# Second attention of a fused block: next queries scaled before the last two tiles' sums, row roots merged with query roots, shared tiles joined in pairs

## What is computed

```
x = x + tanh(g_xattn[0]) * attention0(layernorm(x), ctx)
x = x + tanh(g_ffn[0])   * (routed64(layernorm(x)) + shared(layernorm(x)))
x = x + tanh(g_xattn[1]) * attention1(layernorm(x), ctx)      # the stage changed
x = x + tanh(g_ffn[1])   * mixture8(layernorm(x))

# attention1, 16 heads of 16, keys of 48 + 16 positions, softmax over each part apart
q = ln(x @ Wq + bq);  k = ln(y @ Wk + bk);  v = y @ Wv + bv
ctx = softmax(q k^T / 4) v  +  softmax(q k_dca^T / 4) v_dca
out = ctx @ Wo + bo
```

## Time and profile before

| | us |
|---|---|
| median of 3 runs | 1215.48 (1213.35 to 1218.72) |
| the profiled execution | 1215.52 |
| its span in the trace | 1213.8 |
| busy in it: PE, DVE, ACT, POOL | 953.3, 721.6, 430.7, 279.5 |

### The profile page before, as it was taken

The page is one execution under the profiler, slowest core; times in us unless marked ns, Lnnn a source line. Parts: engine busy times, 40 slices in busy tenths (PEclk is TensorE's granted clock), DMA queues, the critical chain, the costliest instruction groups (busy, mean ns, idle before and its releaser), DMA issues.

```text
span 1213.8 us, 16300 instructions
## 1 busy us (share of the span) xinstructions
PE 953.3 (79%) x5499; PEld 794.4 (65%) x5499; DVE 721.6 (59%) x1685; ACT 430.7 (35%) x809; POOL 279.5 (23%) x225
## 2 busy tenths in 40 slices
PE   5998998989986630576767755777868999999998
PEld 3876867867865520465656632544547989999898
DVE  7267667577478989222222468988986445444343
ACT  4546455454563410111111104355354232332322
POOL 0323303304300000588888720101100000000000
PEclk9999998999989765777787857887869999999899
DMA  8004000000000141578887655000000000000000
GB/s 293 4 1 150 2 1 1 1 1 1 1 1 1 44 123 41 121 167 181 177 184 165 115 132 204 1 3 1 1 1 1 1 18 2 1 17 0 18 1 18
DMA packets 58945, 66.48 MB, mean 55 GB/s; under 512 B 5069, under 2 KB 55687, under 8 KB 58119
## 3 DMA queue, kind: packets, MB, share of 16 engines
q1 hardware_dynamic: 45236, 46.45, 12.4%
q0 software_dynamic: 12288, 18.88, 8.8%
q10 hardware_dynamic: 1363, 0.37, 0.1%
HBM read 48.13 MB, written 17.56 MB: 54 GB/s over the span
## 4 chain that ended last, share of the span: by engine, by line
PE 49%; DVE 19%; issue 13%; DMA 6%; ACT 6%; POOL 6%; ACTq 0%; DVEq 0%; POOLq 0%
PE bank L2039 12%; PE bank L2065 7%; PE bank L1737 4%; DMA acc<-y,dst_now 4%; PE bank L1692 4%; PE bank L1722 3%; PE bank L1926 3%; POOL acc L507 2%; PE bank L2050 2%; DMA xg<-table,src_now 2%; POOL q_lo L486 2%; POOL xg L497 2%; DVE cand L919 2%; PE bank L1713 2%; DVE keyT L922 2%
## 5 line engine op out<-in xcount | busy, mean ns | idle before, releaser
L2039 PE MATMUL bank<-gu_hi,xnT_split 128*128 128x352 f32 x640 | 164.0, 330 | 4.9 <-DVE soft L1235 3.7
L486 POOL TENSOR_TENSOR q_lo<-soft,q_hi 128x512 fp32r<-128x512 f32 x64 | 93.2, 1456 | 237.5 <-ACT soft L1373 237.3
L2039 PEld LDWEIGHTS bank<-gu_hi,xnT_split 128*128 128x128 f32 x640 | 114.7, 192 | 5.6 <-DVE soft L1235 4.0
L507 POOL DMA_INDIRECT acc<-y,dst_now x64 | 102.6, 1603 | 26.8 <-issue 18.3
L2039 PE MATMUL bank<-gu_lo,xnT_split 128*128 128x352 f32 x320 | 104.6, 327 | 0.0
L1235 DVE SCALAR_TENSOR_TENSOR soft<-sg,combine_w,bank 128x176 f32<-128x176 f32 x160 | 56.4, 395 | 70.1 <-PE bank L2039 64.2
L726 DVE COPY qT<-bank 128x512 f32<-128x512 f32 x64 | 44.2, 691 | 88.5 <-PE bank L1737 87.4
L497 POOL DMA_INDIRECT xg<-table,src_now x64 | 64.1, 1002 | 116.8 <-DVE src_now L952 97.6
L972 DVE TENSOR_SCALAR y<-bank,xg 128x256 f32<-128x256 f32 x64 | 28.0, 480 | 103.7 <-PE bank L1854 103.7
L1581 ACT ACTIVATE sg<-bank 128x352 f32<-128x352 f32 x80 | 37.0, 464 | 127.4 <-PE bank L2039 123.3
L1841 PEld LDWEIGHTS bank<-xgT,w_gu 128*88 128x88 f32 x512 | 76.1, 194 | 6.8 <-issue 4.3
(11 more groups left out here) (270 smaller groups left out, 2224.0 us busy)
## 6 DMA issues: line engine op xcount, KB each, us to landing
w_gu<-in_L_ffn_w_gu SPq DMA_DIRECT2D x32, 352.0 KB
w_dn<-in_L_ffn_w_down SPq DMA_DIRECT2D x32, 176.0 KB
acc<-zeros SPq DMA_DIRECT2D x2, 2176.0 KB
acc_rows<-acc SPq DMA_DIRECT2D x8, 512.0 KB, 5.0
gu<-in_L_gu SPq DMA_DIRECT2D x1, 3520.0 KB, 14.7
table<-xw SPq DMA_DIRECT2D x4, 640.0 KB, 3.4
wo<-in_L_xattn_Wo SPq DMA_DIRECT2D x2, 1024.0 KB, 15.5
wq<-in_L_xattn_Wq SPq DMA_DIRECT2D x1, 2048.0 KB, 17.8
```

Of the source, the lines that this page charges most:

```text
L486: pool.tensor_tensor(q2_lo[:, h % 3, :], q2[h % 2], q2_hi[:, h % 3, :], ALU.subtract).then_inc(q2_split, 1)
L507: pool.indirect_dma_start(acc[e], bass.IndirectOffsetOnAxis(ap=dst_now[:, q, e:e + 1], axis=0), y[:, q, e, :], None, compute_op=ALU.add).t ...
L2039: mm = pe.matmul(b[:, 0:2 * F1], v[:, c, j * P:(j + 1) * P], w[:, c, p, o, :], start=(n == 0), stop=(n == len(terms) - 1))
```

## The change

On DVE, `soft2_front` of the next group's tiles 0 and 1 stands at the end of a pass, ahead of the last `attention_out`, and no longer at its start. The deviation and the scaling of the next queries stand ahead of `soft2_back` of tiles 2 and 3. `row_stats` comes before the deviation, `row_roots` is gone in the pass, and its four columns go through the 80 roots' steps as columns 81 to 84. On PE, both outputs 0 and 1 come first, then the next keys and queries, and tile 2's and 3's transposes stand among the next scores. On ACT the order follows, exponentials 0 and 1 stand among the copies of scores, and the loop is written out. POOL's wait for the keys counts four uses of `t_ring` fewer, to fit the new place. The last pass keeps its old order without its first two fronts. Ahead of the stage, the shared expert's tiles are computed and added two at a time, the keys' roots come after eight such tiles and not four, and sums and statistics of later groups stand earlier.

```diff
-                for j in range(G):
-                    residual(NG + i, j, i, 2)
+                for half in range(2):
+                    dve.wait_ge(o_full, G * (NG + i) + 2 * half + 2)
+                    xj = x[:, G * i + 2 * half:G * i + 2 * half + 2, :]
+                    dve.scalar_tensor_tensor(out=xj, in0=o_banks[half][:].rearrange("p (j d) -> p j d", j=2),
+                                             scalar=gates[:, 2:3], in1=xj, op0=ALU.mult,
+                                             op1=ALU.add).then_inc(o_read, 2)
...
+                if rows:
+                    ch.add(dve.tensor_scalar(qk1_stat[:, 0, hi:hi + rows], mv[:, :, 1], EPS0, None, ALU.add))
                 dve.wait_ge(q1_squared, squared)
...
-                inverse_root(qk1_stat[:, 1, lo:hi], v, hi - lo)
+                inverse_root(qk1_stat[:, 1, lo:hi + rows], qk1_stat[:, 0, lo:hi + rows], hi + rows - lo)
...
+            def attention(i, norm):
+                soft2_back(i, 0)
+                soft2_front(i, 2)
+                soft2_back(i, 1)
+                project_keys((i + 1) % 2)
+                soft2_front(i, 3)
+                project_queries()
+                row_stats(norm)
+                deviation(i + 3, rows=G)
+                attention_out(i, 0)
+                scale_keys()
+                scale_queries()
+                soft2_back(i, 2)
+                soft2_back(i, 3)
+                attention_out(i, 1)
+                row_apply(norm, qk1_stat[:, 1, QK:QK + G])
+                attention_out(i, 2)
+                soft2_front(i + 1, 0)
+                soft2_front(i + 1, 1)
+                attention_out(i, 3)
...
             project_keys(0)
             shared_out(0)
+            shared_out(1)
             deviation(1, G * H1, QK)
             scale_keys()
-            for i in range(1, NG):
-                shared_out(i)
+            shared_out(2)
+            shared_out(3)
...
+            dve.wait_ge(acc_used, 2 * NA)
+            row_stats(1)
+            add_up(2)
             project_queries()
+            row_roots(EPS0)
             deviation(2, 0, G * H1)
             scale_queries()
-            dve.wait_ge(acc_used, 2 * NA)
-            normed(1, EPS0)
-            for i in range(2, NG):
-                add_up(i)
+            row_apply(1)
+            add_up(3)
             dve.wait_ge(acc_used, NA * NG)
+            soft2_front(0, 0)
+            soft2_front(0, 1)
...
+                    attn_out(0)
+                    exponential2(i, 2)
+                    attn_out(1)
+                    context_out(0)
+                    exponential2(i, 3)
+                    squares(i + 1)
+                    context_out(1)
+                    keys1_in()
+                    queries1_in()
+                    attn_out(2)
+                    context_out(2)
+                    scores_in(0)
+                    attn_out(3)
+                    context_out(3)
+                    scores_in(1)
+                    exponential2(i + 1, 0)
+                    scores_in(2)
+                    exponential2(i + 1, 1)
+                    scores_in(3)
```

More of the change, by code:

```diff
@@ L1108, in attention @@
                 soft2_front(i, 3)
                 soft2_back(i, 2)
[L1110 to L1114, removed]
+                split_xn(0)
+                split_weights(1)
                 soft2_back(i, 3)
-                if not last:
-                    deviation(i + 3)
                 attention_out(i, 0)
[L1119 to L1123, removed]
@@ L1124, in attention @@
-                attention_out(i, 1)
[L1125 to L1129, removed]
+                split_weights(2)
+                attention_out(i, 1)
+                split_weights(3)
                 attention_out(i, 2)
[L1131 to L1134, removed]
+                split_weights(4)
@@ L1565, in _ @@
             scores_in(0)
-            with act.Fori(0, NG - 1) as i:
+            scores_in(1)
+            exponential2(0, 0)
+            scores_in(2)
+            exponential2(0, 1)
+            scores_in(3)
+            for i in range(NG - 1):
                 attention(i, False)
@@ L1918, in queries1, with scores1 @@
                     mm.then_inc(t_ring.full, 1)
-            def scores1(i):
-                pe.wait_ge(t_ring.free, T4 + TF + TA * i)
-                pe.wait_ge(k_blocks_ready, 4 * (i + 1))
-                for j in range(G):
+            def scores1(i, tiles):
+                if tiles[0] == 0:
+                    pe.wait_ge(t_ring.free, T4 + TF + (TA * i - 4 if i else 0))
+                    pe.wait_ge(k_blocks_ready, 4 * (i + 1))
+                for j in tiles:
                     for c in range(C):
@@ L1986, in attention @@
                 contexts(0)
-                transpose_attn(2)
-                contexts(1)
-                output(0)
-                transpose_attn(3)
-                output(1)
-                contexts(2)
                 if not last:
+                    contexts(1)
+                    output(0)
+                    output(1)
                     keys1(i + 1)
                     queries1(i + 1)
-                contexts(3)
-                output(2)
-                output(3)
-                if not last:
-                    scores1(i + 1)
+                    transpose_attn(2)
+                    contexts(2)
+                    output(2)
+                    scores1(i + 1, (0,))
+                    transpose_attn(3)
+                    contexts(3)
+                    scores1(i + 1, (1,))
+                    output(3)
+                    scores1(i + 1, (2, 3))
+                else:
+                    transpose_attn(2)
+                    contexts(1)
+                    output(0)
+                    transpose_attn(3)
+                    output(1)
+                    contexts(2)
+                    contexts(3)
+                    output(2)
+                    output(3)
             pe.wait_ge(w3_centred, 6)
@@ L2017, in _ @@
             queries1(0)
-            scores1(0)
+            scores1(0, range(G))
             for i in range(NG - 1):
```

100 lines of the change are left out of this document (43 added, 57 removed).

## The result

| | median of the runs (lowest to highest), us | runs |
|---|---|---|
| before, as timed beside the change | 1215.48 (1213.35 to 1219.09) | 5 |
| after | 1221.52 (1220.82 to 1224.63) | 5 |

The ratio from all runs is 1.0053, with a 95% interval of 1.0033 to 1.0073 (the two medians alone give 1.0050): slower, by some 6 us. The profiled execution of the changed kernel took 1224.63 us with a span of 1222.7, the longest of its five; the profiled one of before took 1215.52 with 1213.8.

A forecast was written before the change was run, and what follows sets the result against it. DVE was taken to bound the pass: 36.2 us own work plus 11.0 of waits gave 47.2. Three periods with entry, fronts and last pass ended at 926.8 against 918.6, rounded to 8.0 us later: 1223.5 us, range 1209 to 1229.

The forecast's parts named there:

- DVE's own work: DVE's time in a pass without the new waits, forecast to fall from 44.2 to 36.2 us.
- (a): DVE's wait for ACT's squares, behind exponential 3 and the copies of tile 1 and context 0: 1.5 us a pass.
- (b): POOL's key instructions stretching DVE's multiplication of tile 2's weights: 1.4 us a pass, bounds 0 and 2.0.
- (c): DVE's wait for tile 2's output from PE: 0.4 us at full clock, 3.3 taken at half clock.
- (d): DVE's wait for tile 0's scores behind tile 2's output on PE: 2.0 or 3.6 us by clock, 3.0 taken.
- (e): DVE's wait for tile 1's scores, behind tile 3's transposes, copy and contexts: 1.8 us a pass.
- What the change takes away: From DVE's pass: exponential's wait 2.7, scores' wait 0.6, row roots with their wait 4.9 us; 0.2 us added back.
- The entry: Ahead of the loop: first fronts start at 746.7 instead of 750.28; first scores at about the old time, within 1 us.
- The last pass: The loop's final pass, from its first sums to the end of the last addition, taken over as 32.6 us.
- The clock stays up: Rival, chance 0.30: PE's gap does not lower the clock at tile 2; period 43.3, 1212 us.
- The chain stays off the path: Rival, chance 0.14: waits (c), (d), (e) together under 2 us a pass; period 39.1, 1199 us.
- PE late at a pass's start: Rival, chance 0.06: PE stays at half clock there, DVE waits some 3 us more a pass for projections; 1232 us.

The follow-up runs named there:

- Kernel 3: Changed kernel with POOL spreading only 4 of 64 key positions for groups 1 to 3, same number of instructions; 1218.26 us, ratio to before 1.0023.
- kernel 2: Changed kernel with unused products added on PE, four ahead of the next keys and two behind the queries; 1209.09 us, ratio to before 0.9967.
- kernel 9: Changed kernel with unused products in only PE's first gap, four ahead of the next keys; 1220.05 us, ratio to before 1.0036.
- kernel 10: Changed loop alone, behind the old entry of the kernel before; 1226.36 us, ratio to before 1.0100.
- kernel 5: Kernel before with only row statistics moved ahead of the deviation and row roots merged into the 80 roots; 1217.89 us, ratio 1.0028.
- kernel 11: Kernel before with new entry, exponentials 0 and 1 among score copies, statistics ahead of the deviation and merged row roots; 1208.85 us, ratio 0.9952.
- kernel 12: Changed kernel with the first two score banks ahead of tile 2's transposes on PE, their ACT copies moved likewise; 1208.55 us, ratio 0.9957.
- kernel 8: Kernel before with the new entry, exponentials 0 and 1 among score copies and ACT's loop written out; 1199.63 us, ratio 0.9868.

## Why the prediction was right, step by step

The forecast, 1223.5 us and slower, held: 1221.52, and its cause too. The time lies right at the line of 1221.6 that the prediction drew between slower and no change; that it is slower rests on the interval of the ratio. In its own terms, for a pass, with the second pass of the trace:

| term | predicted | measured |
|---|---|---|
| DVE's own work | 36.2 | 36.3 |
| (a) squares | 1.5 | 1.26 |
| (b) POOL | 1.4 | 1.67 |
| (c) tile 2's output | 3.3 | 3.09 |
| (d) tile 0's scores | 3.0 | 3.73 |
| (e) tile 1's scores | 1.8 | 2.26 |
| period | 47.2 | 48.35 |

DVE's own work is here 48.35 less the five terms, so it holds the short steps between instructions too.

- **What the change takes away** left DVE's own part at 36.3 us, as forecast to a tenth. The step that takes these 8 us out of DVE's pass and then asks what is late next is what decided the case.
- **(b)** was sized at 1.4, between 0 and 2.0, and measured 1.67 in the pair of instructions that it named. Kernel 3 confirms it, 1.6 us a pass in its trace. The Trainium skill, SBUF — State Buffer, SBUF: two separate sides, has such a pair exclude each other for a whole instruction; the trace agrees in that both sides grew, DVE by 1.67 and POOL by 0.90 us. The step that the prediction names as agreeing, at 828.83 in the earlier trace rows, is a weaker witness than it says: it reads one operand, so two operands from SBUF are not what stretched it.
- **(c)** and the clock held as written, half speed for all of PE's chain behind the keys. That the clock makes some 5 of the 9 us of (c), (d) and (e) is shown by kernel 2, whose first two passes have the same order and the same fill. The gap was predicted at over 4 us and was 3.81. The prediction did not list the second one, 2.60 us, though kernel 9 shows that the first one is not needed for the half speed.
- **(d)** was mis-sized: I took 3.0, between 2.0 and 3.6, for a part at full clock. There is none, and it measured 3.73, three times 0.7 us too little.
- **(e)** was 0.5 short, since tile 3's transposes still ran at half clock (1.83 us at 837.73, where the prediction had 1.0).
- **The entry** was 2 us better than the sum (744.56 against 746.7). The prediction started the first front when ACT had made the first copies at the old place; they came 2 us earlier, outside its bounds of 1 us. The two fronts then took 5.04 and not 5.9, since tile 1's scores were there.
- **The last pass** took 34.2 us from its first sums and not 32.6: the additions of tiles 0 and 1 wait 0.65 and 1.93 us for PE, where the old ones waited 0 and 0.75. Order and work of this pass are the old ones without the fronts, and I took its length over as it was. This is not the change's doing each time: in kernel 10, with the same loop, the last pass from first sums to the start of the last addition took 32.15 us as before (32.22), against 33.75 here.
- Together: entry -2.1, fronts -0.9, three periods 144.75 against 141.6, last pass +1.6: 1.7 us later than the sum of 926.8. The last addition ended at 928.58. The medians came out lower than the two traces suggest, at +6.0. That the sum comes so close is in part luck: the entry and the fronts were 3 us too late in it, and the periods and the last pass nearly 5 us too short.
- **The range** has two slips. By its own terms the lower end is 3 x (1.4 + 1.0) less, 1216.3 and not 1217, and the upper end 1223.5 + 3 x (0.6 + 0.6) + 1 = 1228.1 and not 1227.5. Neither changes the forecast.

**The rivals.** *The clock stays up*, 43.3 a pass: kernel 2 shows this pass for once, 42.9 us from one sum of squares to the next (765.72 to 808.65), so the price was right and the condition was not met in the change. *The chain stays off the path*: refuted; even with the clock up the three waits are 3.9 us, over the 2 at which it decides. *PE late at a pass's start*: refuted; the clock is at 1.00 from 840 to 866.

What remains open is why kernel 2's clock stayed up in one pass and not in the next with the same idle times in both; the traces tell what PE did before, and not more. In the change itself the statistics stand in front of a wait of 1.26 us for the squares, so their 2 us there fill time in which DVE would wait for ACT; that they cost as much there as in kernels 5 and 11 is not shown.

## What to carry to other kernels

Work taken off the bound engine is worth only the time until the next thing that engine waits for. Here 4.9 us of row roots mostly covered a wait for PE, and to take them out by moving 2 us of statistics ahead of the keys cost 3 us (kernel 5) or 9 (kernel 11), while a plain wait of 2.7 us in a pass, with no such wait behind it, was worth 9 over the passes. When work is moved ahead of a hand-over to another engine, count what that engine does with the hand-over (idle stretch, clock, first result) before counting what is saved. And put the waiting engine's long independent work (here two banks of scores) ahead of the piece that waits for the slow hand-over: that one reordering took 13 us off the change.

## What the hardware showed beyond the expectation

- An idle stretch of PE of 3.8 us followed by one of 2.6 went with 20 us at 0.50; with the second one filled by needed work the low stretch was about 10 us (kernel 12). Filling only the first one left 14 us at 0.51 (kernel 9). In kernel 2 an idle stretch of 1.50 us in the same place went with full speed in one pass and with 10 us at 0.51 in the next.
- Idle products on PE, whose results nobody reads, made the changed kernel 12 us faster (kernel 2), with a spread over its runs of 9 us. It is still slower than kernel 8, which adds nothing.
- POOL's four key instructions and DVE's two multiplications of two operands from SBUF stretched each other, 4.04 to 4.94 us and 1.29 to 2.96; with POOL's instructions cut to a sixteenth in width, DVE's were back at 1.29.
